# Convolving all heads ahead and merging second block, routing and shared expert into one loop by batches

## The reference

```python
x = x + tanh(g_xattn[0]) * L0_xattn(ln(x), ctx, ctx)      # softmax over k^T q, per batch
x = x + tanh(g_ffn[0])   * L0_ffn(ln(x), W_syn, ...)      # ternary weights, top 102 of 1024 kept per row
x = x + tanh(g_xattn[1]) * L1_xattn(ctx, ctx, ln(x), ...) # long convolution of k*v products, times q
x = x + tanh(g_ffn[1])   * L1_ffn(ln(x), gate_w, ...)     # 64 experts, 6 a row, and a shared expert
```

## Time and profile before

| What | Value |
|---|---|
| median of 3 runs (lowest to highest) | 736.68 us (734.48 to 737.08) |
| profiled execution | 734.65 us |
| span of its profile | 732.9 us |
| PE busy | 613.6 us (84%) |
| DVE, ACT, POOL busy | 474.0, 285.1, 431.6 us (65%, 39%, 59%) |
| DMA | 167.84 MB, mean 229 GB/s |

### The profile page before, as it was taken

The page is one execution under the profiler, slowest core; times in us unless marked ns, Lnnn a source line. Parts: engine busy times, 40 slices in busy tenths (PEclk is TensorE's granted clock), DMA queues, the critical chain, the costliest instruction groups (busy, mean ns, idle before and its releaser), DMA issues.

```text
span 732.9 us, 12157 instructions
## 1 busy us (share of the span) xinstructions
PE 613.6 (84%) x3072; PEld 475.3 (65%) x3072; DVE 474.0 (65%) x1606; ACT 285.1 (39%) x641; POOL 431.6 (59%) x482
## 2 busy tenths in 40 slices
PE   2599995782999956999999649999999999999930
PEld 1355552441888835777777438888888888887720
DVE  3798997999488767688886443444544545454425
ACT  3146677874245522354444403222232323233200
POOL 2487997220254420677777642677677777786660
PEclk9599998897899987999999869999999999999975
DMA  6357665687398945566673469999999999996968
GB/s 215 106 195 255 225 203 182 216 284 290 122 347 314 380 147 185 191 224 214 215 245 129 131 235 293 280 247 260 251 241 255 250 266 264 240 293 112 243 103 311
DMA packets 89035, 167.84 MB, mean 229 GB/s; under 512 B 11280, under 2 KB 53712, under 8 KB 88976
## 3 DMA queue, kind: packets, MB, share of 16 engines
q1 hardware_dynamic: 67504, 138.44, 56.6%
q0 software_dynamic: 20608, 27.82, 19.3%
q10 hardware_dynamic: 864, 0.93, 0.3%
HBM read 93.33 MB, written 73.81 MB: 228 GB/s over the span
## 4 chain that ended last, share of the span: by engine, by line
PE 64%; DVE 13%; issue 9%; DMA 6%; POOL 3%; ACT 2%; SPq 2%; DVEq 1%; POOLq 0%; ACTq 0%
PE psum L1104 11%; PE psum L943 8%; PE psum L1022 6%; PE psum L1117 6%; PE psum L1108 5%; PE psum L1122 4%; PE psum L1088 3%; PE psum L864 3%; PE psum L1033 3%; DVE hh L1680 3%; PE psum L934 2%; PE psum L979 2%; DMA acc<-hh,toki 2%; POOL acc L807 2%; PE psum L896 1%
## 5 line engine op out<-in xcount | busy, mean ns | idle before, releaser
L807 POOL DMA_INDIRECT acc<-hh,toki x128 | 187.9, 1468 | 82.8 <-DVE hh L2025 46.8
L2025 DVE TENSOR_SCALAR hh<-psum,wtok 96x256 f32<-96x256 f32 (+3 forms) x128 | 55.8, 477 | 132.0 <-issue 112.7
L767 POOL DMA_INDIRECT xs_rows<-Z,slot x96 | 96.1, 1001 | 42.2 <-issue 26.0
L1104 PE MATMUL psum<-qT,Z 128*128 128x192 f32 (+3 forms) x480 | 96.8, 345 | 0.0
L1104 PEld LDWEIGHTS psum<-qT,Z 128*128 128x128 f32 x480 | 80.6, 192 | 2.1
L685 POOL TENSOR_TENSOR rstd<-mv,neghalf 128x1 f32<-128x1 f32 (+1 forms) x48 | 33.7, 710 | 74.2 <-DVE mv L1788 59.7
L1373 ACT ACTIVATE qT<-psum 128x384 f32<-128x384 f32 (+3 forms) x64 | 33.5, 523 | 96.7 <-PE psum L1088 95.8
L864 PE MATMUL psum<-wt,hTs 128*128 128x512 f32 x128 | 59.7, 609 | 0.6 <-ACT hTs L1202 0.6
L943 PE MATMUL psum<-wt,hh 128*128 128x256 f32 x256 | 58.6, 383 | 0.0
L1117 PE MATMUL psum<-Z,hh 128*96 128x256 f32 (+3 forms) x240 | 56.7, 379 | 0.0
L1108 PE MATMUL psum<-qT,Z 128*112 128x192 f32 (+3 forms) x240 | 52.2, 340 | 0.0
(11 more groups left out here) (352 smaller groups left out, 1265.6 us busy)
## 6 DMA issues: line engine op xcount, KB each, us to landing
Z<-in_wexp SPq DMA_DIRECT2D x62, 496.0 KB, 4.1
xs_rows<-fill SPq DMA_DIRECT2D x64, 272.0 KB, 3.3
kv_rows<-Z SPq DMA_DIRECT2D x12, 688.0 KB, 3.8
kvb<-kv_rows SPq DMA_DIRECT2D x8, 688.0 KB, 6.2
Z<-co_rows SPq DMA_DIRECT2D x8, 688.0 KB
Z<-kv_rows SPq DMA_DIRECT2D x8, 688.0 KB, 6.3
Z<-xs_rows SPq DMA_DIRECT2D x24, 204.0 KB
Z<-xs_rows SPq DMA_DIRECT2D x16, 272.0 KB
```

The source lines that it names most:

```text
L767: pool.indirect_dma_start(out=xs_rows[:, :], out_offset=bass.IndirectOffsetOnAxis(ap=slot[:, t, k:k + 1], axis=0), in_=H[:, t, :], in_offs ...
L807: pool.indirect_dma_start(out=acc[a][:, :], out_offset=bass.IndirectOffsetOnAxis(ap=toki[0:p, g, j:j + 1], axis=0), in_=y_sb[0:p, s, j, :] ...
L1104: m = pe.matmul(pA[par][:, g * CAP:g * CAP + 2 * p], w[:, s, k, g * P:(g + 1) * P], xT[:, par, k, 0:2 * p], start=(k == 0), stop=(k == 1))
L2025: m = dve.tensor_scalar(y_sb[0:p, s, j, :], pY[par][0:p, j * D:(j + 1) * D], wtok[0:p, g, j:j + 1], None, ALU.mult)
```

## The change

All sixteen heads are convolved in and just behind the threshold stage: 13 (`AHEAD`) before the verdict, the two last-formed heads first and straight from SBUF (`DIRECT`), and three between the first transposes and the first projection of the second block. Four buffers instead of two hold products and Toeplitz matrices. `co_rows` now holds for each pair of batches all heads side by side, so a store has eight runs of 688 bytes per partition where it had one of 5,504; `load_group` reads a pair of batches, all heads, at once. Second block, query products, routing and the shared expert run in one loop of ten iterations: tiles 2v and 2v+1 of the second block, products of batch pair c = v-1, routing of u = v-2, shared expert of w = v-3. `x_rows` is gone, since the routing now goes by batches. Fill rows are stored in the first block (22) and behind the load of the shared weights (42). The first tile of x is loaded and normalised alone, and three small constants are loaded on SP instead of ACT, the bias with the third tile.

```diff
+    NGRP = 2 * NH * 2 * NCOL
+    DIRECT = 2
+    AHEAD = 13
...
-            load_x(0)
+            sp.dma_start(X[:, 0, :], x[0]).then_inc(x_first, 16)
             load_ctx(0, 0)
+            sp.dma_start(X[:, 1:4, :], x[1:4].rearrange("b p d -> p b d")).then_inc(x_in[0], 16)
             load_ctx(1, 1)
...
+            for k in range(NH):
+                if k + 4 < NH:
+                    sp.wait_ge(conv_done, k + 1)
+                    load_toep(k + 4)
+                    if k >= DIRECT:
+                        load_products(k + 4)
+                sp.wait_ge(co_ready, k + 1)
+                sp.dma_start(co_heads[head_of(k)], co[k % 2].rearrange("p (g n) -> p g n", g=NPAIR)).then_inc(co_out[k % 2], 16)
+
+            def load_group(g):
+                if g >= 2:
+                    sp.wait_ge(prod_done, 2 * g - 2)
+                sp.dma_start(groups[g % 2], co_rows[g]).then_inc(kv_in[g % 2], 16)
+
+            for a_ in range(2):
+                sp.wait_ge(co_out[a_], 16 * (NH // 2))
+            load_group(0)
+            load_group(1)
+            sp.dma_start(wsgu_sb, wsgu).then_inc(ws_in, 16)
+            fill_rows(2 * (NT - 5), E)
...
+            for k in range(AHEAD):
+                conv(k)
+            pe.wait_ge(co_ready, AHEAD)
             pe.wait_ge(bad_ready, 1)
             pe.matmul(psum[:, 0, 0:1], onesf[:, :], bad[:, :], start=True, stop=True).then_inc(ones_done, 1)
...
+            conv(AHEAD)
+            turn_hidden(0)
+            turn_hidden(1)
+            conv(AHEAD + 1)
+            project(0)
+            conv(AHEAD + 2)
+            pe.wait_ge(co_ready, NH)
+            pe.wait_ge(ws_in, 64)
+            for v_ in range(NPAIR + 2):
+                c, u, w = v_ - 1, v_ - 2, v_ - 3
+                if u >= 0:
+                    x3_turn(u)
+                if 0 <= c < NPAIR:
+                    turn_q(2 * c)
                 if w >= 0:
                     shared_up(w, 2)
+                if 2 * v_ + 2 < NT:
+                    turn_hidden(2 * v_ + 2)
+                if 2 * v_ + 1 < NT:
+                    project(2 * v_ + 1)
...
+            for v_ in range(NPAIR + 2):
+                c, u, w = v_ - 1, v_ - 2, v_ - 3
+                if 2 * v_ <= NT:
+                    second_block(2 * v_)
                 if w >= 0:
                     shared_hidden(w, 0)
                     shared_hidden(w, 1)
+                if 0 <= c < NPAIR:
+                    times_q(2 * c)
+                    four(2 * c)
                 if u >= 0:
+                    summed = x3_stats(u)
                 if w >= 0:
                     shared_hidden(w, 2)
                 if u >= 0:
+                    x3_moments(u, summed)
+                if 2 * v_ + 1 < NT:
+                    second_block(2 * v_ + 1, u if u >= 0 else None)
+                elif u >= 0:
                     mean_shift(u)
...
+                if 0 <= c < NPAIR:
+                    times_q(2 * c + 1)
+                    four(2 * c + 1)
                 if u >= 0:
                     choose(u)
                     weight_rows(u)
                     place(u)
```

More of the change, by code:

```diff
@@ L312, in build @@
         rows_out = sem("rows_out")
-        kv_in = [sem("kv_in0"), sem("kv_in1")]
+        kv_in = [sem(f"kv_in{a}") for a in range(4)]
         conv_done, co_ready = sem("conv_done"), sem("co_ready")
@@ L383, in build @@
         ctx_in = [sem("ctx_in0"), sem("ctx_in1")]
-        head_in = [sem("head_in0"), sem("head_in1")]
+        head_in = [sem(f"head_in{a}") for a in range(4)]
         tick = {n: sem("tick_" + n) for n in ("pool", "dve", "sp", "pe", "act")}
@@ L426, in load_ctx, with fill_rows @@
                 sp.dma_start(ctxT_s[:, par], ctxT[b].rearrange("(k p) s -> p k s", p=P)).then_inc(ctx_in[par], 16)
+            def fill_rows(first, last):
+                sp.wait_ge(c_done, 1)
+                for e in range(first, last):
+                    sp.dma_start(rows_v[e, 0:CAP, :].rearrange("(p b) d -> p (b d)", b=2),
+                                 fill[:, :, :].rearrange("p b d -> p (b d)")).then_inc(filled, 16)
             def load_ctxH(h):
@@ L770, in scatter, with scatters @@
                     in_=H[:, t, :], in_offset=None).then_inc(scattered, 16)
-            pow_pair(0)
-            for u in range(NPAIR):
-                pool.wait_ge(slots_ready, u + 1)
-                for k in range(K - 1):
-                    scatter(2 * u, k)
-                if u + 1 < NPAIR:
-                    pow_pair(u + 1)
-                scatter(2 * u, K - 1)
-                for k in range(K):
-                    scatter(2 * u + 1, k)
+            def scatters(z, first, last):
+                if 0 <= z < NPAIR:
+                    if first == 0:
+                        pool.wait_ge(slots_ready, z + 1)
+                        pool.wait_ge(c_done, z + 2)
+                    if first == 0 and z == 0:
+                        pool.wait_ge(filled, 16 * (E + 3))
+                    for s_ in range(first, last):
+                        scatter(2 * z + s_ // K, s_ % K)
+            for v_ in range(NPAIR + 3):
+                u, z = v_ - 2, v_ - 3
+                if 0 <= u < NPAIR:
+                    row_numbers(u)
+                scatters(z, 0, 3)
+                if 2 * v_ <= NT:
+                    norm_pows(2 * v_)
+                scatters(z, 3, 7)
+                if 0 <= u < NPAIR:
+                    pow_pair(u)
+                scatters(z, 7, 10)
+                if 2 * v_ + 1 < NT:
+                    norm_pows(2 * v_ + 1)
+                scatters(z, 10, 12)
+                if v_ == NPAIR:
+                    pool.wait_ge(hidT_full, NT)
+                    pool.iota(pid_row[:, :], pattern=[[0, P]], base=0, channel_multiplier=1,
+                              allow_small_or_imprecise_dtypes=True).then_inc(c_done, 1)
             pool.wait_ge(ov_ready, 2)
@@ L1269, in _ @@
             keep_conv(0)
+            keep_conv(1)
+            for a_ in range(2):
+                act.wait_ge(kvq_out[a_], 16)
             act.wait_ge(thr_ready, 3)
@@ L1425, in tiles @@
                 v["at"], v["k"] = start + (hi_ - lo_) * per, 0
-            def run(first, last, body):
-                with dve.Fori(first, last) as t:
-                    body(t).then_inc(v_step, 1)
-                v["k"] += last - first
-                dve.wait_ge(v_step, v["at"] + v["k"])
             def moments(src, t, signal):
@@ L1828, in q @@
+            def times_q(h):
+                g = h // 2
+                dve.wait_ge(kv_in[g % 2], 16 * (3 + g // 2) + 16)
+                dve.wait_ge(qT_ready, h + 1)
+                Y = groups[g % 2].rearrange("p (h m b r) -> p b m h r", h=NH, m=2, b=2)[:, h % 2]
+                qx = qxs[h % 2]
+                R = [prods[:, s // 2, (s % 2) * D:(s % 2 + 1) * D].rearrange("p (l h j) -> p l h j", l=2, h=NH) for s in range(HD)]
                 def q(first):
-                    return qx[:, :, :, h:h + 1, first:first + HD].rearrange("p l (g b) a w -> p (l g) b (a w)", g=2)
+                    return qx[:, :, :, first:first + HD]
```

691 lines of the change are left out of this document (335 added, 356 removed).

## The result

The changed kernel takes 778.72 us (median of 4 runs, 772.92 to 781.91), the kernel before 736.32 beside it: a ratio of 1.0571, 95% interval 1.0505 to 1.0636. It is slower by 42 us, where 773 was forecast in a range of 743 to 792. The profiled execution has a span of 777.1 us against 732.9, 44.2 more. Ratios leave out runs more than 1.5% above the fastest of their kernel (one in experiment 6, two in experiment 10); medians hold them.

| Term | forecast | measured |
|---|---|---|
| start, read where the masks begin | -4 | -1.1 (139.83 for 140.92) |
| threshold stage, from there to the verdict | +10.5 | +11.9 |
| verdict to PE's loop | 35.5 | 37.4 |
| first three iterations | 52 | 51.6 |
| five full iterations | 5 x 27.6 = 138 | 128.9 |

What follows compares the result with a forecast made beforehand. The prediction saw two PE-bound stages, one behind the other, with a seam between them. From 734.65 us, start -4, threshold stage +10.5 and verdict to last place +32 gave 773, range 743 to 792.

Steps and rivals of the forecast that it cites:

- first three iterations: Loop's first three iterations, filling the pipeline: 11, 17.5 and 23.7 us, together 52.
- five full iterations: Loop's steady iterations: a chain of 25.6 us plus 2 for a fallen clock, 27.6 us each.
- The sum: Whole kernel: 734.65 - 4 + 10.5 + 32 = 773 us.
- the last two: Loop's last two iterations, little or no second block but routing: 20.5 us each, 41 together.
- The start: Kernel's beginning: first row tile loaded alone lets statistics start earlier, -4 us (0 to -6); moved fill stores cost 0.
- The threshold stage: Up to the verdict: 13 heads ahead of it instead of 8, 4.5 us per head by DMA, +10.5 us.
- The seam: Between verdict and PE's loop: loop waits for shared weights, starts 35.5 us after the verdict, PE idle 18 us.
- The loop: Ten merged iterations: last place 266.5 us after the verdict, before it was 234.4; +32 us.
- The chain over place, second-block tile and shared product: Each full iteration: DVE's place, tile and product, then PE from shared_up to ranks, sum 25.6 us; PE idles 3.
- The first rival: Loop: wait hidden, DVE sets the pace, its waits under some 7 us (0.7 an iteration); 727 us, chance 0.13.
- The second rival: Threshold stage not stretched (3.5 us a head), clock doesn't fall: 753 us, one alone 763; chance 0.23.
- the third: Threshold stage: short stores slow, every head 5.56 us or more; 785 us, with group loads 792; chance 0.09.

Runs made afterwards that it cites:

- experiment 6: Changed kernel with two shared products moved on DVE ahead of the second-block tile and the third directly behind it: 787.4 us, ratio 1.0686.
- experiment 10: Changed kernel with the late wait for the shared weights, stores in long runs and two shared products early: median 755.9 us, ratio 1.0179.
- experiment 5: Kernel before with the changed start alone (first tile of x loaded and normalised alone, constants on SP's queue): 730.5 us, ratio 0.9941.
- experiment 3: Changed kernel with the first block's 22 fill stores moved behind the load of the shared weights, with the other 42: 777.4 us, ratio 1.0572.
- experiment 12: Kernel of experiment 9 with PE's transposes of tile 2v+3 done twice in four iterations: 775.5 us, ratio 1.0557.
- experiment 4: Changed kernel with the layout of `co_rows` turned, so a head is stored in runs of 5,504 bytes per partition: 771.9 us, ratio 1.0533.
- experiment 8: Changed kernel with 11 heads convolved ahead of the verdict and five behind it, instead of 13 and three: 779.7 us, ratio 1.0591.
- experiment 1: Changed kernel with PE's wait for the shared weights moved from ahead of the loop to the third iteration: 766.2 us, ratio 1.0402.
- Experiments 2: Changed kernel with two shared products moved on DVE ahead of tile 2v of the second block: 777.2 us, ratio 1.0579.
- experiment 9: Kernel of experiment 6 with the third shared product moved inside the second-block tile, ahead of its last aggregate: 781.8 us, ratio 1.0611.

## Why the prediction was right

**The sum** was 38.6 and came to 44.2 in the profiled execution; the start, the five full iterations and the last two differed by 2.9 us and more.

**The start** is the step that failed in its second half: "there PE is busy for 86.6 of 95 us and the DMA share is 0.57, so I take 0 (up to +3)". The first tile alone gives 4.7 us (experiment 5), but with the 22 fill stores one tile's context comes late, by 2.0 to 4.4 us (experiment 3). What of this reaches the masks differs from execution to execution: 3.6 us in this one, none in that of experiment 12. Mean DMA shares say little of one load that queues behind others.

**The threshold stage** came out as worked: 4.5 us a head forecast, 4.6 measured, and the verdict waits for ACT. That the rate of the saturated wait fitted is in part luck: 347 GB/s was no ceiling, since with long stores the stage moved 389, and with short ones 333. What releases a copy is the store of two heads before, and shortening it took a tenth off the pace (experiment 4). The step's consequence was read too simply, though: experiment 8 shows that the verdict's place is worth nothing while the loop waits for the shared weights.

**The seam** was right in mechanism and size (37.4 for 35.5, idle 17.8 for 18), and experiment 1 shows the cause. No row gave the 1.3 us to land; from the group loads to the weights it took 12.3 us where 11.5 were forecast. Its place in the sum is nearly a third of the loss.

**The loop.** The chain over place, second-block tile and shared product is in the trace, and where the clock stays the period is its 25.6 (its terms add to 25.5). That it fits so well is in part luck: there the chain over POOL is the longer one. The clock cost 1.1 us an iteration where it fell (26.8), in two of five, where I had put 2 in all; the five iterations took 9 less. The last two took 7 more: I had priced them by the steady routing and without a fall of the clock, at which shared_down and the pieces of shared_up took 6 us more. The two errors cancel by luck.

**Where my theory was too narrow:** I took the chain for the cost, and expected that without it the period falls. Experiments 2, 6 and 9 take PE's wait away at one place, and it comes back at the next. PE and DVE each have 21.5 us of work and more; what holds the iteration near 25.6 in the traces is that several chains around the loop are equally long, the last of them over POOL's scatters, which I had named for the last two iterations only and not priced. That removing this one too would pay is not shown. The first rival fails by its own condition: DVE's waits are 4 us an iteration, not 0.7. The second rival's unstretched stage and the third's 5.56 us a head are ruled out (4.6); the second's clock came true in three of five iterations.

**Left open:** the 2.1 us after the last place; whether POOL's root of the pair ahead of its scatters, a third buffer for the convolved sums, or a PSUM bank for each of a tile's projections would gain. None was tried.

## What to carry to other kernels

Merging two stages that one engine bounds pays only as far as the next engine's work and its waits allow: here both engines had 21 to 22 us of work in a pair that took 25.5 before and 24.0 to 26.8 after, and two iterations of filling came on top. Put a wait where its data is first used, not ahead of a loop (12.5 us here), and count the transfers ahead of it on its queue. Follow every chain that goes once around a loop, also one over an engine that is not the busiest: to cut one gains nothing while another is as long. When a wait is removed, look at what is late next before counting the gain, and look whether it joins another wait that then is long enough for the clock to fall.

## What the hardware showed that I had not expected

More work on PE made the kernel faster: 0.9 us of transposes in a wait of 2.3 us kept the granted clock at 1.00 and saved 1.7 us an iteration. Single waits of 1.2 to 1.5 us in the steady iterations of experiments 2 and 12 left the clock alone; those of 2.27 us in experiment 9 were followed by 0.54, and of the four of 2.83 to 2.85 us in the changed kernel two were followed by the lower level and two were not. In its last iteration but one, waits of 1.05, 1.53 and 1.53 us within 7 us stood ahead of the shared_down that took 5.49.

Two powers on POOL took 3.77 us in experiment 6. The second began at 314.84, 0.05 us into DVE's row of nine query products, each with two operands in SBUF, and outlasted the row. In experiments 2 and 9 it began 0.4 and 0.2 us into the same row, and the two took 1.37 and 1.18. The Trainium skill, "SBUF — State Buffer", section Terms, has DVE and GpSimd share one pair of SBUF ports, held for a whole instruction while the other blocks. The trace agrees that POOL is blocked in experiment 6, but for a row of instructions, not one (3.2 us against 0.41 for a product); the powers of experiments 2 and 9, and other small POOL operations of 0.24 us, ran in the middle of such a row. Moving the product ahead removed the stall (experiment 9); meeting the row is not enough for it, and what decides stays open.

The runs of the changed kernel spread over 9 us, those of the kernel before over 2.6. In the eleven profiled executions with its first block the first convolution started anywhere from 120.98 to 125.14 us; the wait for the late context, 2.0 to 4.4 us, is part of that.
